# Values with 17 columns per head instead of 32, stored by batch, group, key tile and head

## The reference, cut to what matters

```python
# block 1: attention over the 1024 positions of a batch, 12 heads of 16, with relative positions
qkv = group_norm(x) @ qkv_w + qkv_b
attn = softmax(q * 16**-0.5 @ k.T + rel_h + rel_w)
x = x + (attn @ v) @ proj_w + proj_b
# block 2: attention without positions, then 16 experts of which each token takes one
q, k, v = (layer_norm(t) @ W + b for W, b in ...)
t = t + softmax(q @ k.T / sqrt(192)) @ v
t = t + expert[argmax(layer_norm(t) @ Wg.T + bg)](layer_norm(t))
```

## Time and profile before

| | us |
|---|---|
| timed runs: median of 3 (lowest to highest) | 3111.39 (3110.06 to 3124.24) |
| profiled execution | 3100.89 |
| its span, first to last instruction | 3099.0 |
| PE busy | 2711.8 (88%) |
| DVE busy | 2344.3 (76%) |
| ACT busy | 1938.1 (63%) |
| POOL busy | 909.4 (29%) |
| mean DMA rate | 96 GB/s, 298.41 MB in 210601 packets |

### The profile page before, as it was taken

How to read it: one execution, slowest core, us unless ns; L and a number is a source line. 1 busy time by engine, 2 the same in 40 slices (tenths; PEclk the granted TensorE clock), 3 DMA queues, 4 the chain that set the end, 5 groups by cost and what they waited for, 6 DMA issues and landing times. The chain is left out here.

```text
span 3099.0 us, 57198 instructions
## 1 busy us (share of the span) xinstructions
PE 2711.8 (88%) x20914; PEld 1057.6 (34%) x20914; DVE 2344.3 (76%) x3662; ACT 1938.1 (63%) x3195; POOL 909.4 (29%) x1426
## 2 busy tenths in 40 slices
PE   5887899999999999997799599999999999981787
PEld 3765122222222222221565222222222222270565
DVE  4554799999999999993363699999999999671222
ACT  2443167766766676676344299999999999920333
POOL 0011333333333333321323111111111111045776
PEclk9777599999999999999899699999999999975899
DMA  5777555445445545533466331111111111160221
GB/s 114 216 228 219 106 104 112 102 101 112 102 98 112 105 100 105 110 85 64 117 196 180 109 94 50 50 49 49 50 49 48 48 48 48 50 153 1 59 63 45
DMA packets 210601, 298.41 MB, mean 96 GB/s; under 512 B 59596, under 2 KB 146326, under 8 KB 205746
## 3 DMA queue, kind: packets, MB, share of 16 engines
q0 software_dynamic: 67200, 170.53, 23.5%
q1 hardware_dynamic: 143156, 124.61, 14.9%
HBM read 186.25 MB, written 109.19 MB: 95 GB/s over the span
## 5 line engine op out<-in xcount | busy, mean ns | idle before, releaser
L458 ACT ACTIVATE a_probs<-a_psS 128x1024 f32<-128x1024 f32 x768 | 744.2, 1021 | 381.4 <-PE a_psS L371 381.3
L931 DVE TENSOR_REDUCE a_halfmax<-a_psR 128x2 f32<-128x1024 f32 x768 | 885.9, 1218 | 33.3 <-PE a_psR L759 31.5
L880 ACT ACTIVATE a_probs<-a_psS 128x512 f32<-128x512 f32 x1536 | 835.1, 596 | 89.7 <-PE a_psS L775 65.5
L503 DVE TENSOR_REDUCE h_halfmax<-a_psR 128x1 f32<-128x512 f32 x768 | 490.3, 685 | 48.1 <-PE a_psR L353 43.2
L503 DVE TENSOR_REDUCE a_halfmax<-a_psR 128x1 f32<-128x512 f32 x768 | 492.6, 686 | 39.3 <-PE a_psR L353 34.5
L796 PE MATMUL a_psO<-a_probs,a_v 128*32 128x256 f32 x6144 | 491.4, 391 | 21.0 <-ACT a_outT L862 19.7
L371 PE MATMUL a_psS<-a_qrows,a_krows 121*128 121x512 f16 x1536 | 402.1, 383 | 38.5 <-DMA a_qrows<-relh 37.4
L382 PE MATMUL a_psO<-a_probs,a_v 128*32 128x512 f32 x3072 | 410.1, 606 | 0.6 <-ACT a_probs L458 0.6
L796 PEld LDWEIGHTS a_psO<-a_probs,a_v 128*32 128x32 f32 x6144 | 122.4, 108 | 320.6 <-ACT a_probs L880 264.1
L353 PE MATMUL a_psR<-h_kmax,h_qmax 64*128 64x512 f16 x768 | 178.9, 405 | 21.8 <-POOL h_ident L39 21.5
L371 PEld LDWEIGHTS a_psS<-a_qrows,a_krows 121*128 121x128 f16 x1536 | 120.4, 98 | 225.9 <-DMA a_qrows<-relh 58.2
(11 more groups left out here) (211 smaller groups left out, 3202.9 us busy)
## 6 DMA issues: line engine op xcount, KB each, us to landing
qk<-p_half SPq DMA_DIRECT2D x96, 256.0 KB, 3.4
a_qrows<-rel POOLq DMA_DIRECT2D x96, 256.0 KB, 4.2
a_v<-v POOLq DMA_DIRECT2D x96, 256.0 KB, 3.0
v<-p_v SPq DMA_DIRECT2D x36, 512.0 KB, 6.1
a_qrows<-qk POOLq DMA_DIRECT2D x144, 128.0 KB, 4.8
relh<-p_rel SPq DMA_DIRECT2D x48, 256.0 KB
attn<-a_out SPq DMA_DIRECT2D x96, 128.0 KB, 2.2
rel<-p_rel SPq DMA_DIRECT2D x36, 256.0 KB
```

The source lines that it names most:

```text
L458: nc.scalar.activation(PT[:, blk % 2, 2 * pair:2 * pair + 2, :], psS[:, b0:b0 + 2, :], ACT.Exp, scale=scale).then_inc(exped, 1)
L503: nc.vector.tensor_reduce(mx[:, unit, half:half + 1], psR[:, slot, :], AX.X, ALU.max)\
L880: nc.scalar.activation(PT[:, blk % 2, o, :], psS[:, bank(m), :], ACT.Exp, scale=scale)\
L931: nc.vector.tensor_reduce(MX[:, unit:unit + UNITS // QH // 2 + 1:UNITS // QH // 2, kh], psR[:, slot, :].rearrange("p (r k) -> p r k", r=2) ...
```

## The change

Values keep 17 columns per head, of which the last is the column of ones. `VT` becomes `[128, 2 batches, 3 groups, 8 key tiles, 4 heads, 17]`, so that what one DMA stores is one contiguous piece of 8 x 4 x 17 f32 = 2176 bytes per partition on both sides. The memset fills only the column of ones. VectorE's addition covers one tile of tokens instead of two, so there are two of them for each bank. In the attentions the stationary tile has 17 columns and writes rows 32h to 32h+16 of `psO`. The rows between the heads are written by a new VectorE memset, once per attention; TensorE waits for it (`cleared`) before its first matmul. Where the rows are laid out, `VS` = 32 takes the place of `VW`.

```diff
--- before.py
+++ after.py
@@ -22,7 +22,8 @@
 CC = C // 2
 KT = L // P
 QH = L // 512
-VW = 2 * HD
+VW = HD + 1
+VS = 2 * HD
 REL = HI + WI
 PAIR = 2 * L
 ROUNDS = T // PAIR
@@ -95,6 +96,7 @@
         ring_free = sem("ring_free")
         maxed = sem("maxed")
         otc = sem("otc")
+        cleared = sem("cleared")
         recips = sem("recips")
         paced = sem("paced")
         stored = [sem(f"stored{i}") for i in range(QH)]
@@ -379,7 +381,7 @@
                 if kt == 0:
                     pe.wait_ge(otc, halves + qh + 1)
                 for h in range(GH):
-                    mm = nc.tensor.matmul(psO[32 * h:32 * h + 32, :], V[buf][:, kt, h, :], PT[:, blk % 2, h, :],
+                    mm = nc.tensor.matmul(psO[VS * h:VS * h + VW, :], V[buf][:, kt, h, :], PT[:, blk % 2, h, :],
                                           start=(kt == 0), stop=(kt == KT - 1))
                 mm.then_inc(pvdone, 1)
 
@@ -417,6 +419,7 @@
                         job(jn, j, base, slot(jn), free(jn), u, halves, s + 1)
 
             pe.wait_ge(const_done, 2)
+            pe.wait_ge(cleared, 1)
             if rel:
                 pe.wait_ge(const_km[0], 16 * 6)
             pe.wait_ge(loadedm[0], 16 * NLOADM)
@@ -492,6 +495,7 @@
 
         @block.vector
         def _(dve):
+            nc.vector.memset(psO[:, :], 0.0).then_inc(cleared, 1)
             nc.vector.sem_inc(pvdone, 2)
             nc.vector.sem_inc(ring_free, 3)
 
@@ -515,7 +519,7 @@
                 else:
 
                     qh, half = j[2], steps * QH + j[1] * QH + j[2]
-                    o = psR[:, slot, :].rearrange("p (x v) -> p x v", v=VW)
+                    o = psR[:, slot, :].rearrange("p (x v) -> p x v", v=VS)
                     dve.wait_ge(ring_free, base + jn + 3)
                     nc.vector.reciprocal(RC[:, :, :], o[:, :, HD:HD + 1]).then_inc(recips, 1)
                     dve.wait_ge(recips, half + 1)
@@ -793,7 +798,7 @@
                     pe.wait_ge(otc, halves + qh + 1)
                 cols = slice(256 * part, 256 * part + 256)
                 for h in range(GH):
-                    mm = nc.tensor.matmul(psO[32 * h:32 * h + 32, cols], V[buf][:, kt, h, :],
+                    mm = nc.tensor.matmul(psO[VS * h:VS * h + VW, cols], V[buf][:, kt, h, :],
                                           PT[:, blk % 2, 2 * (h % 2) + h // 2, cols],
                                           start=(kt == 0 and part == 0), stop=(kt == KT - 1 and part == 1))
                 if part == 1:
@@ -938,7 +945,7 @@
                 else:
 
                     qh, half = j[2], s * QH + j[1] * QH + j[2]
-                    o = psR[:, slot, 0:512].rearrange("p (x v) -> p x v", v=VW)
+                    o = psR[:, slot, 0:512].rearrange("p (x v) -> p x v", v=VS)
                     dve.wait_ge(ring_free, base + n + RING)
                     nc.vector.reciprocal(RC[:, :, :], o[:, :, HD:HD + 1]).then_inc(recips, 1)
                     dve.wait_ge(recips, half + 1)
@@ -986,7 +993,7 @@
             return ctx.enter_context(nc.semaphore(f"{name}_{n}"))
 
         def stored():
-            return [sb(f"half{i}", [P, NCH, PAIR], F16) for i in range(2)], sb("v", [P, NT, NH, VW])
+            return [sb(f"half{i}", [P, NCH, PAIR], F16) for i in range(2)], sb("v", [P, 2, NG, KT, GH, VW])
 
         if not first:
             HL, VT = stored()
@@ -1092,8 +1099,7 @@
             engine.sem_inc(gate, 1)
             for b in range(2):
                 for g in range(NG):
-                    engine.dma_start(VN[j * (2 * NG) + (b * NG + g)],
-                                     VT[:, b * KT:b * KT + KT, GH * g:GH * g + GH, :]).then_inc(done, 16)
+                    engine.dma_start(VN[j * (2 * NG) + (b * NG + g)], VT[:, b, g, :, :, :]).then_inc(done, 16)
 
         def store_rows(engine, j, groups):
             engine.wait_ge(rlo, j * NR + (NR // NG if groups[0] == 0 else NR) + 4)
@@ -1391,7 +1397,7 @@
 
         @block.vector
         def _(dve):
-            nc.vector.memset(VT[:, :, :, :], 1.0).then_inc(preset, 1)
+            nc.vector.memset(VT[:, :, :, :, :, HD:VW], 1.0).then_inc(preset, 1)
             nc.vector.sem_inc(vt, 2)
             nc.vector.sem_inc(lo, 1)
             if first:
@@ -1492,10 +1498,13 @@
                     if first and n == 5:
                         low_half(j, 1)
                     dve.wait_ge(vps, j * (NT // 2) + n + 1)
-                    nc.vector.tensor_tensor(
-                        VT[:, 2 * n:2 * n + 2, :, 0:HD].rearrange("p t h d -> p (t h) d"),
-                        psV[:, n % 2, 0:2 * C].rearrange("p (x d) -> p x d", d=HD),
-                        BV2[:, :].rearrange("p (x d) -> p x d", d=HD), ALU.add).then_inc(vt, 1)
+                    b, kt = 2 * n // KT, 2 * n % KT
+                    for t in range(2):
+                        ins = nc.vector.tensor_tensor(
+                            VT[:, b, :, kt + t, :, 0:HD],
+                            psV[:, n % 2, C * t:C * t + C].rearrange("p (g h d) -> p g h d", g=NG, h=GH),
+                            BV2[:, C * t:C * t + C].rearrange("p (g h d) -> p g h d", g=NG, h=GH), ALU.add)
+                    ins.then_inc(vt, 1)
                 if not first:
                     low_half(j, 1)
                 else:
```

## The result

The median of the timed runs falls from 3110.72 to 3073.74 us (before 3105.47 to 3124.24, after 3070.58 to 3081.57, four runs each): ratio 0.9891, 95% interval 0.9866 to 0.9916. In a second session the same two kernels gave 3109.05 and 3073.38, ratio 0.9895 (0.9867 to 0.9923). A gain of over 15.6 us had been given a chance of 0.28. The ratios in this document leave out one slow execution (4163.24 us at a granted clock of 0.553, with only the matmuls changed), without which the median of that kernel would be 3105.36.

A forecast was written before the change was run, and what follows sets the result against it. TensorE was taken to bound the first projection and first attention, VectorE the second attention, with DMA-only tails behind the projections. Terms -4.2 - 5.2 - 5.2 + 2.4 + 0.8 = -11.4 took 3111.4 to 3100.0 us; range 3085 to 3113.

The forecast's parts named there:

- Matmuls on the values, 0: Value matmuls of both attentions: 17-column stationary tiles for 32 save nothing, since the streamed columns set the time; 0 us.
- rival of -8: First attention: weight loads are exposed, so TensorE needs 20 ns less in each of 384 blocks; -8 us, chance 0.14.
- rival of the heads in series: Four value products of each block stop running side by side; +980 us in first attention, some +700 in second, chance 0.02.
- Tail 2, -5.2: DMA stretch behind the second projection: all engines full, 1.475 MB less at 285 to 290 GB/s; -5.2 us.
- The sentence under the rivals: Rival for the value stores: if they stay cut in 512-byte pieces, the forecast sum still stands; no chance of its own.
- Tail 1, -5.2: DMA stretch behind the first projection: eight engines form it and carry 0.74 MB less; -5.2 us.
- the cover: First tail: the eight engines' backlog after the change lasts to 305.6, past SP's last `relh` issues at 301.59.
- Start, -4.2: Start of first projection: the shorter value-tile memset releases the first loads earlier, carried to the projection's end; -4.2 us.
- Clearing, +2.4: Start of each attention: TensorE's first matmul waits for the output bank's memset, 1.2 us per attention; +2.4 us.
- Additions, +0.8: Additions writing the values: 64 become 128 smaller ones, a pair costs 0.05 us more, 16 times; +0.8 us.
- SyncE's stores in the other rounds, 0: SP's value stores outside the last rounds become shorter to issue, letting second-projection loads and addition come earlier; costed at 0.
- The overlap that the step named: Second projection: POOL's addition lies over a VectorE low half; 4.2 us may come off or on once or twice, costed at 0.

## Why the prediction was wrong, step by step

- **Matmuls on the values, 0: wrong, and the largest error of reasoning.** The step said that the second attention "is held by VectorE; nothing comes of it there". The row it rests on has TensorE at 902.84 of 946 us and VectorE at 894.95: neither held the stage alone, and the step read only the second. The four profiles with 32 columns loaded give 969.4 to 970.3 us, the ten with 17 give 963.5 to 964.5. A weight load takes 95 ns for 108. The rule that the Trainium skill gives ("TensorE: Matmul & The Clock Gate", section "LDWEIGHTS (loading the stationary operand)"), time in proportion to the columns, gives as an estimate 12.5 ns less for 15 columns; the trace has 13. The durations themselves are far above what it gives, 108 and 95 ns for some 27 and 14. In the first attention, where I had looked for exposed loads as a rival of -8, the means are 1136.2 (32) and 1133.5 (17), but the ten with 17 spread from 1130.3 to 1138.5: a gain there is not shown. The rival of the heads in series is refuted by the same numbers: an output of 17 rows keeps the four heads side by side.
- **Tail 2, -5.2: right place, mis-sized, measured -8.3, for a reason that the step did not have.** It divided the bytes saved by a rate. What the layout did was to merge eight pieces into one, which also made POOL's six issues 2.0 us shorter. Tail 2 by piece and bytes: 512 B, 3.15 MB 15.6 to 16.0; 272 B, 1.67 MB 14.9; 4096 B, 3.15 MB 10.9; 2176 B, 1.67 MB 6.8 to 7.6; none 3.3. The sentence under the rivals, "if the stores stay cut in 512-byte pieces, the bytes still fall, and the sum stands", is false: of 8.3 us 0.7 would have stood. At fewer pieces the bytes do count, 3.4 us from 10.9 to 7.5. The rate in the second tail of after is that of before (289 for 290), which looks like bytes over rate; the kernel with half the bytes in 272-byte pieces (181 to 202) shows that the rate was no constant to divide by.
- **Tail 1, -5.2: the eight engines held, the cover did not; measured -3.1, and -3.2 over four profiles that store as before and four as after (18.3, 15.1).** The stores of row terms take half of the share. But their backlog, said to last until 305.6, was gone at 298 (share 0.31), so the tail became the time that the last row terms themselves take, and removing the values changes no more (14.9). Nor is it the bytes alone that emptied the engines: with all bytes of before in long pieces the tail is 15.4, with half of them in 272-byte pieces 13.3.
- **Start, -4.2: right in the chain (-4.3 at TensorE's first matmul, -4.0 at the second eviction).** At the end of the projection -4.0 and -2.0 remain. The five kernels with the long or half memset load the activation table at 30.3 to 33.5, seven of the nine others at 29.2 to 29.7, two at 32.2 and 33.1 for reasons that no run isolates. In those two (without the last values, and with the row terms on 16 engines) the projection ends at 303.0 and 302.5, later than in before: the gain of the start can be lost whole.
- **Clearing, +2.4: wrong, under 0.1 each.** VectorE starts 0.2 us behind POOL in the later attention, not 1.35. The first has the same order of events, and its start moved by the same 6.1 us as POOL's identity.
- **Additions, +0.8: not measured.** With one addition for two, the second projection took 275.2 us, longer than in any kernel with two (269.3 to 272.8), with a long low half of VectorE beside POOL's addition. A term of 0.8 cannot be seen beside that.
- **SyncE's stores in the other rounds, 0: -1.1, within the spread.** The overlap that the step named is there, and the second projection differs by 5 us between two kernels whose projections are the same (271.6 and 276.8). The step let it come off or on, and this bears it out.
- **Not in the sum at all: routing, -6.2.** A stage behind the change, whose instructions are the same, waits for 64 scatters of 128 x 4 bytes, and how long depends on where the arrays lie in DRAM. No row of before could have given the number.

Still open: the two profiles of each differ by 29.0 on average, the timed medians by 37.0 and 35.7. Before's profiled executions (3100.9 and 3101.8) lie at the lower edge of its timed ones (3098.66 to 3125.7), after's (3074.2, 3070.0) within theirs. Where before's other runs lose some 9 us more, no profile of before shows; a second projection that is 5 us longer, as in the profile with the slots first, is a candidate. The mechanism behind the address effect is not shown either, only that size and place of the arrays switch it.

## What to carry to other kernels

Price a store by its pieces as well as its bytes: a full share of the DMA engines went here with anything from 181 to 369 GB/s, and an order of the tile that merges the pieces was worth more (4.8 us) than halving the data in as many pieces (0.7). In a stage where two engines are 95% busy each, neither alone holds it: read the one wait that repeats in each period before a change to either is costed at 0. And when a change resizes arrays in DRAM, compare the stages behind it too, scattered writes above all, before the whole difference is put down to the edit.

## What the runs showed of the hardware that I had not expected

- 272-byte pieces took the DMA engines nearly as long as 512-byte ones (tail 14.9 for 15.6 to 16.0 us, at 181 to 202 GB/s and a share of 1); 4096-byte ones went at 316 to 342 GB/s, and the last row terms, spread over all 16 engines, at 362 to 369.
- Moving one 4-byte-per-token array to another place in DRAM changed the landing of its scatter from 15.4 to 10.9 us; shrinking two other arrays, to 8.2 to 9.5.
- SyncE took 1.6 us to issue each of its last stores behind the stores of values, 0.8 without them. That full queues are the reason is not shown.
- POOL's time to issue six stores followed their pieces and not their bytes: 5.26 and 5.27 us for pieces of 272 and 512 bytes, 3.27 and 3.21 for 2176 and 4096.
- A matmul output of 17 rows that starts at row 32h ran beside its three neighbours as one of 32 rows does.
- A low half of VectorE took 2.35 us where it began 1.4 us before POOL's addition and 7.87 where it began 1.0 us after it.
- Of two loads issued 3.2 us apart at the start (x at 5.38 and at 8.58), the data were there at the same time (20.26 and 20.37); issued at 2.60 they came at 15.4 to 16.8.
